# A sorting network on VectorE: one payload move placed between the maximum and the minimum of its neighbour

## The reference

```python
for i in range(E):                                   # E = 16, K = 384, D = 768
    gate_feature = hidden_states * pe[i] @ gate_w + gate_b
    gate_weight, gate_idx = jax.lax.top_k(gate_feature, K)
    gate_weight = jax.nn.softmax(gate_weight, axis=-1)
    gathered = jnp.take_along_axis(hidden_states, gate_idx, axis=-1)
    y = y + _moe_mlp(gathered * gate_weight, eg_w[i], eu_w[i], ed_w[i])
```

## Time and profile before

| | before |
|---|---|
| median of three runs | 7316.7 us |
| the profiled execution, its own time | 7314.8 us |
| its span | 7313.0 us |
| VectorE busy | 5625.4 us, 77% |
| TensorE matmul busy | 6048.6 us, 83% |
| GpSimd busy | 3137.3 us, 43% |
| ScalarE busy | 2711.6 us, 37% |
| mean granted TensorE clock | 0.938 of full speed |

### The profile page before, as it was taken

One profiled execution on the slowest core, in us unless ns is written; L12 is line 12 of the kernel. 1 busy time (PEld: TensorE's weight loads), 2 busy tenths in 40 slices (PEclk: granted clock), 3 DMA queues, 4 the chain that ended last, 5 costly groups with the idle time before them and its releaser, 6 DMA issues. The chain is left out here.

```text
span 7313.0 us, 76698 instructions
## 1 busy us (share of the span) xinstructions
PE 6048.6 (83%) x16985; PEld 3132.3 (43%) x16985; DVE 5625.4 (77%) x6713; ACT 2711.6 (37%) x4185; POOL 3137.3 (43%) x3512
## 2 busy tenths in 40 slices
PE   7989988888787878787878787878787878788888
PEld 5545544444343434343434343434343434344454
DVE  3011012999899989898999898999999999998860
ACT  0000000444444444444444444444444444444341
POOL 2233033545454545354545454545454545454440
PEclk9989999999999989899999899999999999999999
DMA  3355364000000000000000000000000000000101
GB/s 87 115 150 147 116 141 135 20 14 14 14 14 14 14 14 14 14 14 14 14 14 14 14 14 14 14 14 14 14 14 14 14 14 14 14 14 14 59 20 47
DMA packets 118210, 262.95 MB, mean 36 GB/s; under 512 B 39164, under 2 KB 49922, under 8 KB 117682
## 3 DMA queue, kind: packets, MB, share of 16 engines
q1 hardware_dynamic: 70322, 180.18, 6.9%
q0 software_dynamic: 47360, 77.17, 4.7%
HBM read 222.43 MB, written 34.58 MB: 35 GB/s over the span
## 5 line engine op out<-in xcount | busy, mean ns | idle before, releaser
L1107 PE MATMUL mask_ps<-key,neg_ident 125*125 125x480 f32 (+7 forms) x4128 | 1929.0, 588 | 717.8 <-DVE key L1383 711.5
L1309 ACT COPY mask_ps<-key 125x960 f32<-125x960 f32 (+7 forms) x1136 | 952.5, 838 | 1762.8 <-DVE pay L1425 1383.8
L1205 POOL TENSOR_TENSOR pay<-pay_rest,pay 125x360 int32<-125x360 int32 (+11 forms) x1104 | 882.0, 799 | 1472.8 <-DVE pay L1408 1471.0
L1107 PEld LDWEIGHTS mask_ps<-key,neg_ident 125*125 125x125 f32 x4128 | 745.0, 196 | 1680.7 <-DVE key L1383 1203.4
L1408 DVE COPY_PREDICATED pay<-mask_ps,pay 125x480 f32<-125x480 int32 (+5 forms) x1104 | 1229.8, 1114 | 116.8 <-PE mask_ps L1107 80.1
L1198 POOL TENSOR_TENSOR pay_rest<-pay 125x360 int32<-125x360 int32 (+11 forms) x1104 | 878.1, 795 | 812.4 <-DVE pay L1425 512.2
L1374 DVE TENSOR_TENSOR key<-mask_ps,key 125x480 f32<-125x480 f32 (+5 forms) x1104 | 1084.4, 982 | 40.4 <-PE mask_ps L1107 35.0
L1383 DVE TENSOR_TENSOR key<-mask_ps,key 125x480 f32<-125x480 f32 (+5 forms) x1104 | 1087.7, 985 | 8.3
L1107 PE MATMUL mask_ps<-key_top,neg_ident 125*125 125x480 f32 (+3 forms) x1472 | 613.7, 543 | 317.9 <-DVE key_top L1383 303.8
L1425 DVE COPY_PREDICATED pay<-mask_ps,pay_rest 125x600 f32<-125x600 int32 (+9 forms) x1104 | 832.2, 754 | 39.7
L1323 ACT COPY pay_rest<-pay 125x600 f32<-125x600 f32 (+9 forms) x1104 | 678.6, 615 | 425.3 <-DVE pay L1425 232.6
(11 more groups left out here) (178 smaller groups left out, 5855.2 us busy)
## 6 DMA issues: line engine op xcount, KB each, us to landing
w_rel<-L_gnn_W SPq DMA_DIRECT2D x16, 2304.0 KB, 23.4
w_exp<-L_ffn_ed_w SPq DMA_DIRECT2D x16, 2304.0 KB, 8.4
messages_dram<-y_out SPq DMA_DIRECT2D x16, 1875.0 KB
w_exp<-L_ffn_eg_w SPq DMA_DIRECT2D x16, 1152.0 KB, 5.3
w_exp<-L_ffn_eu_w SPq DMA_DIRECT2D x16, 1152.0 KB, 7.8
root_w<-L_gnn_root SPq DMA_DIRECT2D x2, 2304.0 KB
w_exp<-L_ffn_sg_w SPq DMA_DIRECT2D x4, 1152.0 KB, 5.8
w_exp<-L_ffn_su_w SPq DMA_DIRECT2D x4, 1152.0 KB, 8.5
```

Source lines behind the costliest of these rows:

```text
L1107: last = pe.matmul(mask, neg_ident[0:TP, 0:TP], operand, start=False, stop=True, skip_group_check=True)
L1205: pool.tensor_tensor(second, shares(pay_was(u))[1].bitcast(I32), first, ALU.subtract).then_inc(pays_taken, 1)
L1309: act.copy(seed_of(u), compared(u)[0]).then_inc(seeded, 1)
```

## The change

In the second half of the network, a unit that is the first of two in its stage gets another order on VectorE: the first move of the unit before it now stands between the maximum and the minimum, where it stood behind the minimum. All other units keep their order, and no other engine's program is altered.

```diff
                 for u in range(FIRST[APART], NU):
                     larger_keys(i, u)
-                    smaller_keys(i, u)
-                    first_pays(i, u - 1)
+                    if UNITS[u][1:] == (0, 2):
+                        first_pays(i, u - 1)
+                        smaller_keys(i, u)
+                    else:
+                        smaller_keys(i, u)
+                        first_pays(i, u - 1)
                     if u == NU - 1:
                         top_key(i)
                     second_pays(i, u - 1)
```

## The result

| | before | changed |
|---|---|---|
| median, with the range of the runs | 7319.99 us (7311.38 to 7327.55, 6 runs) | 7394.45 us (7377.26 to 7410.54, 6 runs) |
| profiled execution, its own time | 7314.8 us | 7405.9 us |
| its span | 7313.0 us | 7404.1 us |

The ratio is 1.0100, with a 95% interval of 1.0084 to 1.0116: about 75 us slower. The length of an execution goes with the mean granted clock of TensorE: of the six executions of the changed kernel, the three with a clock of 0.942 took 7377 to 7385 us, and the three with 0.935 to 0.937 took 7403 to 7411 us. The profiled one is of the upper three, so what its trace shows adds up to 91 us, not to the 75 us of the medians.

A forecast was written before the change was run, and what follows sets the result against it. VectorE and TensorE were taken as level from unit 56 on, tied at the maxima. 54 us (3.35 a sort, sixteen sorts) plus 20 us for the clock, on 7314.8, gave 7390 us, 1.0% slower; eight-in-ten range 7340 to 7430.

The forecast's parts named there:

- The tie at unit 58: Maximum of 58, 0.14 us behind unit 57's mask, is tied to TensorE; 56 to 58 goes 9.06 to 10.25 us.
- The slice behind the delayed mask: On TensorE the delayed first mask pushes its slice and the second unit's mask; cost 1.2 us at unit 56.
- The cost at unit 59: Late GpSimd sum and longer first move delay the minimum; the maximum of 61 comes 1.3 us later.
- The seams: VectorE's three gaps between operations go from +0.10 to about -0.30 us, gaining 0.39 us a place where VectorE alone decides.
- third rival: VectorE's gaps are alike in both orders, so delays grow by about 0.25 us; 7427 us, chance 5%.
- Units 63, 65, 67, 71 and 91: Costs a sort of 0.5, 0.35, 0.25, 0.25 and 0.3 us, in that order, without the clock.
- Unit 61: No slice stands behind its mask, so the delay finds cover and a gain of 0.4 us stays.
- the cover of the delayed first mask: The first unit's mask, delayed with its minimum, isn't wanted for another 3 us, so its delay itself costs nothing.
- The clock: Longer TensorE idle before the masks of 59 and 65 brings more falls to 1.2 GHz: +20 us, bounds -29 to +53.
- The range: Eight in ten for 7340 to 7430 us, the upper end called halfway into the third and fourth rivals' times.
- third and fourth rivals' times: 7427 us with gaps alike in both orders, chance 5%; 7424 us with the clock at its upper bound, chance 14%.

## Why the prediction was right

The forecast of 7390 and the measured 7394.5 agree, and so do direction and range. The mechanism at the places is right too. That the number fits to 5 us is luck in part: the terms of the clock are off in both directions, and the six executions alone lie 33 us apart. Point by point:

- **The tie at unit 58.** Right. It now shows as an idle of 1.44 us released by TensorE, and 56 to 58 at full clock is 10.1 us instead of the predicted 10.25.
- **The slice behind the delayed mask.** Right, and shown at unit 56 at full clock: from the maximum of 56 to that of 58 it takes 10.12 us with the slice behind the mask, 8.70 with it ahead. With the slices ahead of the masks and nothing else changed, 91 us go, but the clock's part is in that. The cost at unit 59 apart from the clock is 1.2 to 1.4 us against the predicted 1.3.
- **The seams.** Right in size. At full clock a place with its slice out of the way gives 0.37 (56 to 58, 9.07 to 8.70, slices ahead in both). So the third rival, by which the seams are alike in both orders, does not hold here. The two seams with a signal differ from those without by 0.12 and 0.28 us in the rows before, where the prediction says 0.1 to 0.2. Whether the signal or the kind of the neighbour makes a seam long, no run separates.
- **Units 63, 65, 67, 71 and 91.** Right within about 0.2 us. At 65 this holds only after the clock is taken off: the mask took 3.48 instead of 1.88, which is 1.60 of the 1.94.
- **Unit 61.** Wrong: the gain of 0.4 came out as 0. The step that failed is the cover of the delayed first mask. At 61 the first move of that unit had to wait for it (the mask ends at 4447.96 + 1.88 = 4449.84, the move starts at 4450.35), and a move held by a mask starts 0.51 us after it, not 0.14. At unit 59 in the same sort the move starts 0.52 after its mask.

```profile
4447.96 1.88 PE L1107 MATMUL mask_ps<-key,neg_ident 125*125 125x480 f32 x4 [1.05 <-DVE key L1383]
...
4450.35 1.24 DVE L1408 COPY_PREDICATED pay<-mask_ps,pay 125x960 f32<-125x960 int32 x1 [0.31 <-issue]
```

  In `first_pays`, further waits and semaphore steps stand behind the wait for the mask, and in `larger_keys` the wait for the mask is the last. That VectorE takes the further ones only once the first is over would explain the 0.37 us; no run tests it.
- **The clock.** Right in sign, mis-sized in its parts. I took +20 us. At 59 and 65 it cost 1.6 us a sort each (2.87 - 1.3 and 3.48 - 1.88), about 45 us over the loop in the profiled execution, and at 56, where I had nothing for it, 0.5 (10.59 - 10.12). The step that failed is reckoning each place by itself: at 69 to 71 a fall went away (0.6 us a sort), and in the last expert, where TensorE was late already, 56 to 92 became 2.8 us shorter instead of longer. The good agreement of the total owes something to these cancelling.
- **The range.** The upper bound of 7430 was called halfway into the third and fourth rivals' times, but it lies above both (7427 and 7424).

The order of the reasons, then: the pushed mask of the second unit is shown at its places, by the run with the slices ahead. That the clock's falls at 59 and 65 come from the longer idle ahead of them is supported by their disappearance when the slices fill it (8.12 and 8.05 us). It isn't shown, for single-place runs moved falls to untouched units too, and at 65 with an idle time that hadn't changed. How the 75 us divide between mask and clock stays open: at 56 alone, the pushed mask cost 1.04 us a sort at its place and nothing in the total.

## What to carry to other kernels

When an operation is moved on one engine, look at what is queued behind its consumer on the next engine, not only at whether the consumer itself has time. Here most delayed masks had cover (2.6 us at unit 56, about 1 at 61), and the work behind them had none. The cure lay on that engine: work that needs nothing can go ahead of an instruction that waits, where the engine is idle in front of it. Where it is not, this costs: 0.5 us at unit 63 in the old order, and some 7 us in the last expert. And where the clock of TensorE falls now and then, judge an edit of half a microsecond by the whole kernel, with a control that has the other half of the edit, because falls gained at one place are often paid at another. With that control, moving the slices was worth 18 and 43 us by itself in two runs and nothing in the third, and the new order gave 22 us, 2 us and -12 us.

## What the runs showed of the hardware that I had not expected

- Being busy was not enough to hold the clock. With 2.84 us of bias products (contraction over one row) and no idle time between them and the mask, the granted clock fell to 0.50 in ten of fourteen sorts, as often as with 2.54 us of idle in their place. With the slice itself in the gap (one bias product, then products over 128 rows), 59 to 61 stayed at 8.1 us in all sorts.
- Falls of the clock move. The new order at 69 alone took the fall at 70 away, and others appeared between 65 and 67, 10.11 us on average instead of 8.44, where no instruction and no idle time ahead of the mask (2.69 us) had changed.
- A maximum, whose last wait is the one for a mask, starts 0.14 us after it. A first move, which has further waits behind the one for its mask, starts 0.51 us after it.
- Two neighbouring VectorE operations, where the second waits for the first's signal, are 0.03 to 0.15 us apart. Without such a wait the second starts 0.07 to 0.13 us before the recorded end of the first.
